# Scan of a test-time-trained layer on one core: a new order of one turn's operations on TensorE, VectorE and GpSimd, and single waits for single parameters

## The reference

```
x = x + 0.5 * ffn(layernorm(x))         # 8 experts, top 2, and a shared one
x = x + attn(layernorm(x))
x = x + 0.5 * ffn(layernorm(x))

def attn(x):
    k, v = split(x @ W_KV)
    def step(params, (k_t, v_t)):        # one step for each of 1,024 times
        g = grad(mean((silu(k_t @ W1 + b1) @ W2 + b2 - v_t) ** 2))
        return params - 0.001 * g
    W1, b1, W2, b2 = scan(step, (W1, b1, W2, b2), (k, v))
    return silu(x @ W_Q @ W1 + b1) @ W2 + b2
```

## Time and profile before

| | |
|---|---|
| median of 3 runs | 485.08 us (483.19 to 486.23) |
| the profiled execution, its time | 484.08 us |
| its span in the trace | 481.9 us |
| granted TensorE clock, mean | 0.947 of 2.4 GHz |
| TensorE matmul busy | 430.7 us (89%), 2875 instructions |
| TensorE weight loads busy | 356.0 us (74%) |
| VectorE / ScalarE / GpSimd busy | 280.8 / 245.1 / 243.1 us |

### The profile page before, as it was taken

The page is one execution under the profiler, slowest core; times in us unless marked ns, Lnnn a source line. Parts: engine busy times, 40 slices in busy tenths (PEclk is TensorE's granted clock), DMA queues, the critical chain, the costliest instruction groups (busy, mean ns, idle before and its releaser), DMA issues.

```text
span 481.9 us, 9866 instructions
## 1 busy us (share of the span) xinstructions
PE 430.7 (89%) x2875; PEld 356.0 (74%) x2875; DVE 280.8 (58%) x1031; ACT 245.1 (51%) x617; POOL 243.1 (50%) x369
## 2 busy tenths in 40 slices
PE   7899899999908989999999999999799799999940
PEld 5444699999903679899999989974644499999930
DVE  4945455555528646677777777754965245555514
ACT  3594355555410445556556565544696145555520
POOL 4367777545500344555555546552247777554530
PEclk9799999999957999999999999999989999999985
DMA  8981334100075200000000000000001417110028
GB/s 231 260 278 56 113 104 151 37 26 25 18 186 175 41 1 0 3 2 2 1 2 1 1 2 2 3 0 1 2 23 56 112 50 205 35 34 28 20 63 216
DMA packets 34513, 30.89 MB, mean 64 GB/s; under 512 B 3838, under 2 KB 30085, under 8 KB 34464
## 3 DMA queue, kind: packets, MB, share of 16 engines
q1 hardware_dynamic: 24608, 19.17, 14.7%
q0 software_dynamic: 4544, 8.47, 5.4%
q10 hardware_dynamic: 5312, 2.62, 2.1%
HBM read 15.55 MB, written 15.61 MB: 65 GB/s over the span
## 4 chain that ended last, share of the span: by engine, by line
PE 73%; DVE 8%; DMA 6%; POOL 4%; issue 4%; ACT 4%; ACTq 0%; SPq 0%; DVEq 0%; POOLq 0%
PE bank L1308 18%; PE bank L741 15%; PE bank L728 14%; POOL slots_dram L1435 3%; PE bank L599 3%; DMA stage<-y_dram 3%; PE bank L1101 2%; PE bank L689 2%; PE bank L716 2%; PE bank L1178 2%; DMA stage<-slots_dram 2%; PE bank L1139 1%; DVE stats L419 1%; PE bank L699 1%; PE bank L1162 1%
## 5 line engine op out<-in xcount | busy, mean ns | idle before, releaser
L1692 DVE TENSOR_TENSOR sq<-bank,relu 128x512 f32<-128x512 f32 x86 | 59.5, 692 | 84.2 <-ACT relu L839 84.0
L1440 POOL DMA_INDIRECT y_dram<-y_out,stage x78 | 76.9, 986 | 59.2 <-ACT y_out L865 52.6
L741 PE MATMUL bank<-proj_w,sq 128*128 x624 | 86.4, 281 | 2.8 <-DVE sq L1692 2.8
L728 PE MATMUL bank<-tileT,tile_w 128*128 128x128 f32 x624 | 83.2, 277 | 0.0
L1435 POOL DMA_INDIRECT slots_dram<-rows,slots x64 | 63.3, 990 | 35.0 <-DVE slots L535 15.2
L741 PEld LDWEIGHTS bank<-proj_w,sq 128*128 128x128 f32 x624 | 75.6, 191 | 6.5 <-issue 3.5
L839 ACT ACTIVATE relu<-bank 128x512 f32<-128x512 f32 x94 | 56.1, 596 | 45.4 <-PE bank L728 37.6
L728 PEld LDWEIGHTS bank<-tileT,tile_w 128*128 128x128 f32 x624 | 76.9, 195 | 0.0
L865 ACT ACTIVATE y_out<-bank,stage 128x128 f32<-128x128 f32 x78 | 28.7, 368 | 33.2 <-PE bank L741 33.2
L1303 POOL TENSOR_TENSOR sq<-sq,last_rows 128x128 f32<-128x128 f32 x32 | 14.7, 458 | 54.2 <-DVE sq L1279 54.2
L599 PE MATMUL bank<-ones 128*128 128x512 f32 x32 | 20.6, 790 | 15.4 <-DVE res L1743 12.6
(11 more groups left out here) (278 smaller groups left out, 1046.6 us busy)
## 6 DMA issues: line engine op xcount, KB each, us to landing
slots_dram<-pad SPq DMA_DIRECT2D x2, 2535.0 KB, 14.0
stage<-slots_dram SPq DMA_DIRECT2D x18, 260.0 KB, 4.4
fc_w<-experts SPq DMA_DIRECT2D x1, 2048.0 KB, 20.3
proj_w<-experts SPq DMA_DIRECT2D x1, 2048.0 KB, 24.0
stage<-y_dram SPq DMA_DIRECT2D x8, 256.0 KB, 5.5
stage<-y_dram ACTq DMA_DIRECT2D x8, 256.0 KB, 6.2
y_dram<-y_out,stage POOLq DMA_INDIRECT x78, 2.3
res<-x SPq DMA_DIRECT2D x4, 256.0 KB, 3.8
```

The source lines that it names most:

```text
L728: last = nc.tensor.matmul(bank[i % 2][:, f_cols], tile_w[:, i % 2, f_cols], tileT[:, (f * NQ + tile_q(i)) % 2, tile_cols(i)], start=True, ...
L741: last = nc.tensor.matmul(bank[4 + i % 2][:, 0:P], sq[:, i % 2, f_cols], proj_w[:, k, f_cols], start=j == 0, stop=j == FJ - 1)
L1440: nc.gpsimd.indirect_dma_start(y_dram.ap(), bass.IndirectOffsetOnAxis(tiles[:, t, P:P + 1].bitcast(U32), 0), y_out[:, t % YBUFS, :], None, ...
L1692: nc.vector.tensor_tensor(wide_of(i)[2], wide_of(i)[0][:], wide_of(i)[1], ALU.mult)\
```

## The change

The loop bodies of TensorE, VectorE and GpSimd are written in another order; ScalarE's stays as it was. No operation on data is added or left out. On TensorE, the transpose of `e` of `early[1]` moves from the start of the next turn to the end of its own, `pe_yrows` goes ahead of `pe_aa` (and for `early[1]` also ahead of `pe_y` and `pe_da_old` of `late[1]`), `pe_a_transposed` of `late[0]` behind `pe_y`, and `pe_first` of `late[1]` from the middle of `late[0]` to its end. On VectorE `d` and `ee` of `early[1]` follow each other directly behind the update of w1, and the parameter updates come in the order b2, b1_half, w2t, b1, w2. On GpSimd the additions of squares move from before the slopes of the first iterations to behind them. Each parameter update is a function with waits of its own for its sums and, in the chain `ahead`, for the final parameter that it starts from. In the built program VectorE's list for the scan is 56 instructions longer, all of them waits. The core of the diff:

```diff
-        PARAMS = ("w1", "b1_half", "b1", "b2", "w2t", "w2", "ahead_w1", "ahead_b1_half", "ahead_b1", "ahead_b2",
-                  "ahead_w2t", "ahead_w2")
-        LAST_PARAMS = ("w1", "b1_half", "b1", "b2", "w2t", "w2")
+        PARAMS = ("w1", "b2", "b1_half", "w2t", "b1", "w2",
+                  "ahead_w1", "ahead_b2", "ahead_w2t", "ahead_w2", "ahead_b1_half", "ahead_b1")
+        LAST_PARAMS = ("w1", "b2", "b1_half", "w2t", "b1", "w2")
...
                 if turn:
                     square_gap(turn)
-                    add_gap(turn)
                 pool_slope(pool, late[0])
+                if early:
+                    pool_slope(pool, early[0])
                 if turn:
                     square_new(turn)
-                if early:
-                    pool_slope(pool, early[0])
-                if turn:
+                    add_gap(turn)
                     add_new(turn)
...
+            def final_made(turn, name):
+
+                if turn >= 0:
+                    dve.wait_ge(params_done, params_at(turn + 1, name))
...
+            def dve_ahead_b1(turn):
+                dve.wait_ge(ahead_upd1, turn + 2)
+                final_made(turn, "b1")
+                moved_by(ahead.b1, ahead.d_bank[:, P:P + 1], 0.5 * GRAD, final.b1)
...
                 dve_w1(turn)
+                if early:
+                    dve_d(dve, early[1])
+                    dve_ee(dve, early[1])
+                dve_b2(turn)
+                dve_b1_half(turn)
+                dve_w2t(turn)
                 dve_b1(turn)
-                if early:
-                    dve_d(dve, early[1])
-                dve_b2(turn)
-                if early:
-                    dve_ee(dve, early[1])
-                dve_w2()
...
                 pe_da(pe, late[0])
+                pe_e_transposed(pe, late[0])
                 if early:
                     pe_inner(pe, early[0])
-                pe_e_transposed(pe, late[0])
                 pe_ee(pe, late[0])
+                pe_first(pe, late[1], turn)
                 pe_again(pe, late[1])
```

More of the change, by code:

```diff
@@ L1491, in _ @@
                 if turn:
+                    square_new(turn)
+                    add_gap(turn)
                     add_new(turn)
[L1493 to L1497 removed]
+                pool_slope(pool, late[1])
+                if early:
+                    pool_slope(pool, early[1])
+                gap_of_last(turn)
             for part in (square_gap, add_gap, square_new, add_new):
@@ L1970, in _ @@
                 pe_y(pe, late[0], turn)
+                pe_a_transposed(pe, late[0], turn)
                 pe_th_transposed(pe, late[0])
-                pe_first(pe, late[1], turn)
                 if early:
@@ L1977, in _ @@
                 if early:
+                    pe_yrows(pe, early[0], turn)
                     pe_y(pe, early[0], turn)
[L1979 removed]
                 pe_da_old(pe, late[0])
```

107 lines of the change are left out of this document (56 added, 51 removed).

## The result

| | before | after |
|---|---|---|
| median | 484.91 us (483.19 to 486.23, 4 runs) | 478.70 us (477.20 to 479.02, 4 runs) |
| ratio, 95% interval | | 0.987 (0.983 to 0.991) |
| the profiled execution, time / span | 484.08 / 481.9 us | 479.02 / 477.1 us |
| a turn, w1 update to w1 update, median of 13 | 9.29 us | 8.94 us |
| the last turn | 8.76 us | 8.79 us |

The forecast was 479.7 us. A second measurement of the changed kernel gave 477.94 us against 484.40, 0.988 (0.985 to 0.990).

The account below looks back on a forecast made before the run. Bound: the two exact iterations' dependent chain, 8.75 of 9.3 us a turn, with TensorE's queue standing still about 1.5. 14 x 0.37 plus 0.2, 5.4 us, off 484.08 gives 478.7; the median stands 1.0 higher: 479.7, range 477.0 to 484.6.

Parts of the forecast that it names:

- the first leg: From the load of the final w1 sums to `late[0]`'s inner matmul: 4.06 us before, 3.78 forecast, 0.28 shorter.
- the walk: Working one turn forward, instruction by instruction, from trace timings: 9.32 us for the old order, 8.93 for the new.
- The second leg: From `late[0]`'s inner matmul to the next w1 sums: 5.23 us before, 5.15 forecast, 0.08 shorter.
- the tie at its end: GpSimd's slope and TensorE's `da` of `late[1]` finish together; before, the slope was done 0.15 us ahead.
- Rival (a): GpSimd's slope of `late[1]` sets the turn: 0.14 us longer there, turn 9.15, 483.0 us; chance 0.25, shared with similar losses.
- VectorE's waits: Ten waits each turn gains on VectorE, for counts long reached: taken to cost nothing.
- Rival (c): Waits make VectorE's updates the bound: at 0.1 us each the turn is 0.46 us longer, 491.5 us; chance 0.05.
- GpSimd's order: Additions of squares behind the first iterations' slopes end 0.46 us before `late[1]`'s `u` comes: no cost.
- rival (b): TensorE's weight loads can't be packed closer, filled waits show up again behind, time stays at 485; chance 0.1.
- The Trainium skill's rule: TensorE's limit read by weight loads' busy share, 91%: at most 9% of a turn, 0.84 us, could be won.
- The sum: 14 turns x 0.37 = 5.2 us, turn 0 another 0.2, the last turn 0.0: total gain 5.4 us.

Follow-up runs that it names:

- e1: The kernel before with only TensorE's new order; median 480.76 us, ratio 0.993, turn 9.083 us.
- e2: The kernel before with only VectorE's new order, its waits and the new parameter order; median 485.85 us, ratio 1.006, turn 9.417 us.
- e5: The changed kernel with TensorE's order where one turn meets the next put back as before; profiled execution 482.82 us, turn 9.246 us.
- e9: The changed kernel with a small GpSimd memset ahead of the slope of `late[1]`; profiled execution 481.46 us, turn 8.967 us.
- e4: The kernel before in its old order, with separate waits ahead of VectorE's parameter updates; profiled execution 483.87 us, turn 9.293 us.
- e3: The kernel before with only GpSimd's new order; profiled execution 482.88 us, turn 9.291 us.
- e10: The kernel before with a small GpSimd memset ahead of the slope of `late[1]`; profiled execution 483.38 us, turn 9.284 us.
- e12: The changed kernel itself, measured once more; median of 5 477.94 us, ratio to before 0.988, turn 8.942 us.
- e11: The changed kernel with three more moves on TensorE; median of 6 477.78 us, ratio to before 0.987, turn 8.912 us.
- e7: The changed kernel with the transpose of `th` of `late[1]` put back behind `pe_y_last`; profiled execution 479.18 us, turn 8.943 us.

## Why the prediction was right

**The turn.** 8.93 forecast, 8.94 measured. Both legs came out: 3.78 and 5.15 forecast, 3.80 and 5.14 at the seam shown (3.78 and 5.15 at another). In the first, `d` and `ee` of `early[1]` start 0.90 and 1.11 us behind the w1 sums (0.90 and 1.10 forecast), `pe_again` and `ahead`'s sums are loaded at 1.37 and 1.51 (1.37 and 1.48; the sums 0.14 behind `pe_again`, not 0.11). That the first leg's gain needs both engines' orders at once, as the walk had it, is shown by e1, e2 and e5: without VectorE's part 0.12 of 0.27 us are left, without TensorE's seam nothing.

**The second leg.** Its length was right, and so was the tie at its end, but that the length fits to 0.01 us is luck. Of `late[1]`, `e` starts at 3.62 us (forecast 3.70), `da` is loaded at 4.19 (4.27), the slope ends at 4.70 (4.80), `d` starts at 4.80 (4.82). So both ends of the tie came 0.07 to 0.10 us ahead of the walk, 0.01 apart; but `d` started 0.10 us behind the end of the slope, where the walk had put 0.02. Two errors cancelled: had `d` followed GpSimd as fast as it follows TensorE (0.04 us), the leg would have been some 0.06 shorter. In the kernel before that handover didn't show, since `da` came last there. By e9 0.05 us more on the slope cost 0.03. Rival (a), the slope taking over, was thus the right mechanism with a price near zero, and not the 0.22 us that it was given. What kept it small is what the prediction said against it: before, `u` waited for ScalarE's rows until 3.88 us into the leg, 0.14 later than `e` would have let it. `e` came 0.15 us later, and that used up just this room: `u` starts at 3.88 again, now behind `e`.

**VectorE's waits.** Taken at nothing: e4 and the rows at 251.24 to 251.57 show it. Rival (c) falls as a price of every turn (0.7 us), and of the ten waits only some four a turn are instructions of their own (56 in 14 turns), so that its own 0.07 us apiece would have made 0.3; its path, through `ahead`'s b1 to `early[0]`'s silu, is real and carries the long turns 7 and 10, with a slack of 0.10 us and not 0.17 (last section). **GpSimd's order**: nothing, by e3 and e1. **A full queue**, rival (b), falls: 637 loads in a stretch that had 614. The Trainium skill's rule (Perfetto Trace Analysis, § Identifying the Most-Contended Engine) reads such a stretch by the busy share of the loads, beside a share of the peak rate of operations: the busy share has gone from 91 to 94% (76.23 of 81.40 us), so that 91% still left room for a turn 4% shorter, within the 9% that the prediction read from the rule. (DMA, which the prediction has at nothing there, moves 2 GB/s in both; nothing rests on it.)

**The sum.** For the 15 steps from the w1 update of turn 0 to that of turn 15, 14 x 0.37 + 0.0 = 5.2 us were forecast; they took 139.11 us before and 134.47 after, 4.64 us less. The 0.55 that are missing are the three long turns (0.08 + 0.09 + 0.14 = 0.3), 0.03 of the last turn, and 0.356 rounded up to 0.37 (0.2). The sum has no term for long turns; the prediction didn't see them. Turn 0 by itself, from the first update of `ahead`'s w1 to that of w1, took 9.76 us before and 8.09 after; but in e3, e4 and e10, with the old order on TensorE and VectorE, it took 8.29 to 8.33, so that the order is worth the forecast 0.2 there, and the rest is the clock, below. In the pair of profiles the part ahead of the scan was 1.9 us longer after than before, which cancels it.

So 4.8 us are found in the scan. The medians say 6.2 (by the interval 4.6 to 8.2) and, measured again, 6.5 (4.8 to 7.1). What lies beyond 4.8 isn't explained; three medians of the kernel before alone were 484.91, 483.96 and 484.40 us, so that 1 us of it is no more than their scatter. Some of it seems to go with the clock. Of the 11 executions of the kernel before that were taken beside e12, eight had a mean granted clock of 0.944 to 0.948 and took 484.22 to 486.17 us, three had 0.954 to 0.958 and took 482.68 to 482.90; the five of e12 had 0.951 to 0.960. Those three (median 482.88) stand 4.9 us above e12's median. Whether the new order makes the lower clock rarer isn't shown. The forecast of 479.7 came out 1.0 above the median.

## What to carry to other kernels

Where one engine's queue is full and in order, write down the start of each of its instructions over one turn, find the few gaps over the bare spacing, and move work that is ready into them; such a walk, set against the trace of before first, gave the length of a turn of 70 loads to 0.01 us, though single steps of it were off by 0.10; it missed three quarters of a gain once two waits ran within 0.1 us of each other (e11). Ask of every wait what came second: a move that takes the last one away (`e` in e7) gains only as far as the next. An order is one package across engines: half of it can be worth nothing, or less. Compare small changes by the step of the loop in the trace, not by the time of the whole.
